# Layer 1 of a two-layer graph network: the gathered rows are added to the edge attributes by the transfer itself

## The reference, cut to what matters

```python
m = node_feat[src] + edge_feat                      # 200000 x 128
neigh = jax.ops.segment_sum(m, dst, num_segments=N)
h = 2.0 * node_feat + neigh
h = h @ W1 + b1
h = jnp.where(h > 0, h, 0.01 * h)
x = _layernorm(x + h @ W2 + b2)
```

## Time and profile before

| | us |
|---|---|
| median of 3 runs | 5750.64 (5744.35 to 5753.44) |
| span of the profiled execution, first to last instruction | 5652.3 |
| what lies around the span, if the profiled execution took the median's time | 98.3 |
| mean granted clock of PE, share of 2.4 GHz | 0.783 |

### The profile page before, as it was taken

One profiled execution on the slowest core, in us unless ns is written; L12 is line 12 of the kernel. 1 busy time (PEld: TensorE's weight loads), 2 busy tenths in 40 slices (PEclk: granted clock), 3 DMA queues, 4 the chain that ended last, 5 costly groups with the idle time before them and its releaser, 6 DMA issues. The chain is left out here.

```text
span 5652.3 us, 80469 instructions
## 1 busy us (share of the span) xinstructions
PE 3416.6 (60%) x19294; PEld 2795.9 (49%) x19295; DVE 2121.7 (38%) x8176; ACT 1585.3 (28%) x3447; POOL 2973.6 (53%) x3194
## 2 busy tenths in 40 slices
PE   5667676766666766767666455545555555555554
PEld 4455454545445544545544444445455455545454
DVE  4454554545544544545545122222222222222222
ACT  3343443334333433334333111111111111111111
POOL 2454454544554554555552656555555565555554
PEclk8787888778887878778877677777777777777777
DMA  7333333333333333333332533333333333333332
GB/s 227 81 97 89 91 94 86 93 82 92 92 88 86 94 87 86 90 85 95 91 88 59 102 91 93 92 90 93 92 92 93 92 93 92 93 91 93 92 93 70
DMA packets 459582, 525.88 MB, mean 93 GB/s; under 512 B 199115, under 2 KB 359287, under 8 KB 459551
## 3 DMA queue, kind: packets, MB, share of 16 engines
q1 hardware_dynamic: 266498, 268.35, 16.3%
q0 software_dynamic: 100352, 208.93, 15.3%
q10 hardware_dynamic: 92701, 48.23, 3.0%
HBM read 471.23 MB, written 53.95 MB: 93 GB/s over the span
## 5 line engine op out<-in xcount | busy, mean ns | idle before, releaser
L671 POOL DMA_INDIRECT rows<-xl_table,src_idx x1568 | 1482.2, 945 | 1458.0 <-DVE wmsg L1124 655.5
L1446 POOL DMA_INDIRECT rows<-x_table,src_idx x1568 | 1480.4, 944 | 1102.7 <-issue 605.8
L1491 PE MATMUL ph<-ident,relu_h 128*128 128x128 f32 x196 | 83.9, 428 | 1103.0 <-DVE relu_h L1636 726.0
L1491 PEld LDWEIGHTS ph<-ident,relu_h 128*128 128x128 f32 x196 | 33.0, 168 | 1164.0 <-DVE relu_h L1636 755.5
L703 PE MATMUL ph<-node_of,xr_win 128*128 128x512 f32 x784 | 517.8, 797 | 5.9 <-issue 5.1
L745 PE MATMUL pA<-wmsg,edge_of 128*128 128x136 f32 x3136 | 430.7, 293 | 94.9 <-issue 56.9
L911 ACT ACTIVATE relu_h<-ph 128x512 f32<-128x512 f32 x392 | 232.1, 597 | 849.3 <-PE ph L703 551.9
L1532 ACT ACTIVATE relu_h<-ph,b 128x128 f32<-128x128 f32 x196 | 72.0, 367 | 1383.6 <-PE ph L1496 1044.1
L745 PEld LDWEIGHTS pA<-wmsg,edge_of 128*128 128x128 f32 x3136 | 402.7, 199 | 104.8 <-issue 100.5
L767 PE MATMUL pA<-win,last_node 128*1 128x136 f32 x392 | 99.0, 345 | 573.7 <-ACT win L925 513.1
L729 PE MATMUL pT<-att_heads,relu_h 128*128 128x48 f32 x3136 | 383.6, 272 | 79.0 <-issue 52.5
(11 more groups left out here) (174 smaller groups left out, 6322.4 us busy)
## 6 DMA issues: line engine op xcount, KB each, us to landing
dst_row<-in_dst SPq DMA_DIRECT2D x196, 513.0 KB
dst_row<-in_edge_attr SPq DMA_DIRECT2D x195, 512.0 KB
rows<-xl_table,src_idx POOLq DMA_INDIRECT x1568
rows<-x_table,src_idx POOLq DMA_INDIRECT x1568
sums_table<-win ACTq DMA_DIRECT2D x196, 68.0 KB
xr_win<-xr_table SPq DMA_DIRECT2D x196, 64.0 KB
relu_h<-x_table SPq DMA_DIRECT2D x196, 64.0 KB
out_x<-relu_h ACTq DMA_DIRECT2D x196, 64.0 KB
```

What stands on the lines that cost most here:

```text
L671: pool.indirect_dma_start(rows[s][:, t, :], None, xl_table[:, :], bass.IndirectOffsetOnAxis(ap=src_idx[s][:, t:t + 1], axis=0))\
L1446: pool.indirect_dma_start(rows[s][:, t, 0:D], None, x1_table[:, :], bass.IndirectOffsetOnAxis(ap=src_idx[s][:, t:t + 1], axis=0))\
L1491: pe.transpose(across_bank, x1_slot[s], ident[:, :]).then_inc(S("x1_across"), 1)
```

## The change

In layer 1 the gathers write to `attr` and add to what stands there; PE multiplies only `attr`. For that POOL waits for the attributes of the group as well as for its indices. The indices are loaded one group earlier, and SP waits for the gathers that read the slot's earlier indices before it loads new ones. The indices of group 3 too are loaded at the end of layer 0.

```diff
-                for s in range(BACK):
+                for s in range(U):
                     sp.wait_ge(S(f"rows_free0{s}"), groups // U + 1)
                     sp.dma_start(src_idx[s][:, :], bass.AP(a["src"].tensor, s * G, [[T, P], [1, T]]))\
                       .then_inc(S(f"src_in1{s}"), 16)
...
+                def load_sources(g):
+                    s = g.c % U
+                    wait_alone(sp, sp_waits, S(f"gathered1{s}"), g.use(16 * T, 0))
+                    sp.dma_start(src_idx[s][:, :], bass.AP(a["src"].tensor, g.times(G), [[T, P], [1, T]]))\
+                      .then_inc(S(f"src_in1{s}"), 16)
+
                 def load(g, parts=P):
                     s = g.c % U
                     sp.wait_ge(S("neigh_summed"), g.times(1, 1))
-                    if g.at_least(BACK):
-                        sp.dma_start(src_idx[s][:, :], bass.AP(a["src"].tensor, g.times(G), [[T, P], [1, T]]))\
-                          .then_inc(S(f"src_in1{s}"), 16)
...
                 def step(g, near):
+                    if g.at_least(U - 1) and in_range(g + 1, groups):
+                        load_sources(g + 1)
...
                         wait_alone(pool, pool_waits, S(f"src_in1{s}"), j * 16 + 16)
+                        wait_alone(pool, pool_waits, S(f"attr_in{s}"), j * 16 + 16)
                         for t in range(T):
-                            pool.indirect_dma_start(rows[s][:, t, 0:D], None, x1_table[:, :],
-                                                    bass.IndirectOffsetOnAxis(ap=src_idx[s][:, t:t + 1], axis=0))\
+                            pool.indirect_dma_start(attr[s][:, t, :], None, x1_table[:, :],
+                                                    bass.IndirectOffsetOnAxis(ap=src_idx[s][:, t:t + 1], axis=0),
+                                                    compute_op=ALU.add)\
                                 .then_inc(S(f"gathered1{s}"), 16)
...
-                    for k, m in enumerate((attr[s], rows[s][:, :, 0:D])):
-                        for t in range(T):
-                            ins = pe.matmul(bank, m[:, t, :], one_hot[:, t, :], start=(k == 0 and t == 0),
-                                            stop=(k == 1 and t == T - 1))
+                    for t in range(T):
+                        ins = pe.matmul(bank, attr[s][:, t, :], one_hot[:, t, :], start=(t == 0), stop=(t == T - 1))
...
-                    wait_alone(pe, pe_waits, S(f"attr_in{s}"), g.use(16, 16))
                     wait_alone(pe, pe_waits, S(f"gathered1{s}"), g.use(16 * T, 16 * T))
```

More of the change, by code:

```diff
@@ L1378, in _ @@
                 left_over(v, "v0l", rest_steps, homes[:, spots:spots + 2], SPAN)
-        end_phase(*[f"src_in1{s}" for s in range(BACK)])
+        end_phase(*[f"src_in1{s}" for s in range(U)])
         stat = [sb(f"stat{s}", [P, 2, 12]) for s in range(R)]
```

## The result

The changed kernel took 6058.43 us (median of 4 runs, 6041.08 to 6060.18), the kernel before on the same chip 5747.5 us (5736.91 to 5753.44): ratio 1.0506, interval 1.0469 to 1.0543. It is 5% slower where 8% faster was forecast, and lies above the stated range, which ended at 5930 us. The profiled execution took 6060.18 us.

A forecast was written before the change was run, and what follows sets the result against it. It took the PE, DVE, PE chain (12.85 us a group) as bound, then POOL: start 3128 plus 196 x 10.45 = 2048, a tail to 5197, plus 98.3 around the span: 5295 us, 456 less; range 5185 to 5930.

The forecast's parts named there:

- The adding form's price on POOL: POOL's time for an adding gather in layer 1: between 0.944 and 1.42 us, the lower end taken.
- Rival 2: POOL describes three ends of each row for two: 1.42 us a gather, 13.7 us a group, 5920 us; chance 0.12.
- anything else above 5930: The bracket for all times over 5930 us, beyond the stated range; chance 0.17, shared with rival 3.
- rival 3: DMA engines don't overlap reading and adding, one round trip a gather: 16 us a group, 6370 us; chance 0.17 with its bracket.
- further issue gaps: POOL's issue idle time in layer 1 beyond 0.30 us a gather: 0.50 us a group, kept in the 10.45 us.
- Rival 1: POOL's adding instruction grows moderately, to 1.0 to 1.3 us; 157 us for each 0.1: 5340 to 5740 us; chance 0.18.
- The DMA engines' part: The gathers' queue: a second read makes 0.276 us a gather 0.41 to 0.55, hidden under POOL's 1.244.
- PE's chain: PE, DVE, PE in layer 1: 12.85 us a group falls to 7.92 or 9.86 with half the passes, under POOL's 9.95.
- Rival 4: PE stays the bound, its sum slow for a reason other than the number of passes: 5750 us, no change; chance 0.03.
- The waits: POOL's wait for attributes and SP's for `gathered1`: free with POOL as bound, except a start 19 us later.
- The 98.3 us around the span: Difference between the kernel's median time and its traced span before, added to the 5197 us span to give 5295.
- The signs named in advance: Profile after: gather ns, POOL over 70% busy, few `src_idx` waits, 16 records, PE waiting, clock under 0.76, `add` every 10.0 to 10.8 us.

The follow-up runs named there:

- add_two_sets: The kernel before with its gathers adding into their old buffer `rows`, PE still multiplying both sets: 6041.76 us, 14.84 us a group.
- forms: The changed kernel with four adding and four plain gathers a group, of 128, 64 and 32 full rows and 128 rows of 256 bytes: 5560.12 us.
- plain_one_set: The changed kernel with plain gathers to `rows`, its waits kept, PE multiplying `rows` alone: 5854.34 us, ratio 1.017 to the kernel before.
- dve_merge: The changed kernel with plain gathers to `rows`; DVE adds `rows` to `attr` before PE multiplies one set: 5782.18 us, ratio 1.0038 to the kernel before.
- narrow_rows: plain_one_set with gathered rows of 64 bytes in place of 512: 5838.07 us.
- two_sets_fill_272: The kernel before with only a POOL fill of 128 x 272 elements after each gather: 5622.17 us, ratio 0.9768.
- merge_fill_272: dve_merge with a POOL fill of 128 x 272 elements after each gather and fewer waits on fills: 5625.34 us, ratio 0.975 to the kernel before.
- merge_paced_1: dve_merge with a POOL fill of 128 x 136 elements after each gather: 5628.36 us, ratio 0.9936 to the kernel before.
- merge_paced_half: dve_merge with a POOL fill of 128 x 136 elements after every second gather: 5660.53 us.
- merge_fill_200: dve_merge with a POOL fill of 128 x 200 elements after each gather and fewer waits on fills: 5591.97 us, ratio 0.9724 to the kernel before.
- merge_sequencer: dve_merge without a fill, ten already satisfied semaphore waits before each gather on POOL: 5826.27 us.

## Why the prediction was wrong, step by step

**The adding form's price on POOL: the term that was mis-sized, and the one that decided.** The prediction bounded it by 0.944 and 1.42 us and took the lower end. It measured 1.550 us, beyond the upper end; a group of eight is 14.84 us where the forecast had 10.45, and the point of no gain, 1.31 us, was passed. Rival 2 had the place right, POOL's instruction, and the size too small: 13.7 us a group, and its 5920 us was 138 us short. The time fell into the bracket of 0.17 for "anything else above 5930", whose named cause, rival 3, didn't come. add_two_sets shows that this alone makes the time. Whether POOL's extra time is a third end to describe, as that rival said, isn't shown, and the shapes in forms speak for nothing so simple. Bytes and rows of the gather were indeed the same; that they would fix POOL's time was the error.

A second term, 0.50 us a group of further issue gaps, was kept in the forecast and left out of the rivals. With it rival 2 would have read 6018 us, and the range would have reached near what was measured. But that would have been luck: 14.84 us is 8 x (1.550 + 0.304), so the 0.50 us were nothing when POOL didn't wait. Rival 1's 5340 to 5740 us doesn't follow from its own 157 us for 0.1 either: from 5295 at 0.944 it gives 5383 to 5853.

**The DMA engines' part was right.** The adding gathers' packets are 144 each, (275968 - 1568 x 32) / 1568, where a plain one has 32 (100352 / 3136). Their time is 21.2% of 6058.3 us less 1568 x 0.276, 852 us, that is 0.543 us a gather for 0.276: twice, within the 0.41 to 0.55 of the prediction, and hidden behind POOL's 1.855. The 0.276 is the mean of both layers; the packets of 3300 to 5300 us alone give 0.249 plain and 0.547 adding, 2.2 times. The Trainium skill says of the collectives' reduce step that it reads two sources for each chunk and for that runs at about half a copy's rate (Collectives: The Full Stack, "The bandwidth ceiling"); the measured ratio is near this. The price lay on the engine that issues. Rival 3 fell.

**PE's chain: the step that failed in its reasoning.** "If the 9.86 us are in proportion to the passes" they fall to 4.93, and by the recorded 2.99 us at least to 6.87. plain_one_set and dve_merge have half the passes and groups of 13.6 and about 13.3 us. From the same rows the prediction had read that the sum comes 5.4 us after the records, and had priced this gap as PE's work. With adding gathers and all 32 passes (add_two_sets) the gap is 0.19 us in every group. So it isn't the passes; it is time in which the news of PE's end is held up while POOL issues closely spaced gathers. Rival 4 had said so (a reason other than the number of passes), got 0.03, and its reason against it, the recorded 2.99 us, wasn't one. With the price of the adding form as forecast, the change would have brought about nothing, or a loss, if these two runs stand for it: dve_merge 1.0038, plain_one_set 1.017. In the change as made this doesn't show, because its own gathers are 1.855 us apart.

**The waits were costed right, for POOL as the bound.** POOL waits for attributes once, before the first gather. The 91.9 us there are mostly the end of layer 0; the attributes' part is 17.6 us (the gather starts 17.8 us after SP's first attribute issue, 0.2 before), where the forecast had 19. That the start at 3128 was measured at 3130.6 is partly luck, since the end of layer 0 varies by more. SP's wait for `gathered1` and the earlier indices cost nothing, with the cover named. In plain_one_set, where POOL isn't the bound, POOL waits 732.8 us for attributes, mostly after a late release.

**The 98.3 us around the span don't exist.** The changed kernel's span is 1.9 us short of its execution's time, and in every profiled run of the study they are at most 2.0 us apart. So the profiled execution of before took some 5654 us, less than the median of its kernel, and the prediction's own sum should have read 5199 us, not 5295: a small error beside the others. More follows from it: the traced execution is faster than every timed one beside the changed kernel (5736.91 to 5753.44 us), so the 12.85 us a group are those of a fast execution. If all of the difference lies in layer 1, the usual pace before is some 13.3 us (an estimate: 12.85 + 94 / 196), and the loss is 1.5 us a group, not 2.0.

**The signs named in advance** came mostly true (not the 10.0 to 10.8 us from `add` to `add`): the gathers' mean ns told the rival at once, POOL was busy 84% of the stretch, no wait for `src_idx`, 16 records a group, PE waiting for the gathers, and a granted clock of 0.55 for 0.76, which is a mean just above the lower level of 1.2 GHz, after waits of some 8 us before each sum.

**What is open.** Which part of the chip POOL's gathers and PE's completion share. Shown is that the hold-up ends with POOL's run in plain_one_set and narrow_rows and doesn't depend on the bytes (narrow_rows). With one set it vanishes with distance: by the earlier of SP and DVE the release is late by 15.6 us at 90% of the groups in dve_merge (1.245 us from gather to gather), 9.8 at 1.345 and 8.8 at 1.40, and not late at all with fills of 272 columns and more. It isn't each single distance that counts, since forms has close gathers and no lag; whether it is the mean pace or what the gathers have to describe isn't separated. The kernel before has a lag too, but it doesn't always last until POOL stops: of 168 late releases 74 came while POOL was still gathering. With two sets the lag is gone at 1.855 us (add_two_sets), but 6.5 us are left at 1.45 (two_sets_fill_272). Whether the lag with two sets is the same hold-up wasn't settled. The granted clock isn't the cause: from 4000 to 4200 us it is 0.62 in plain_one_set, where PE is late, and 0.59 in merge_fill_272, where it is on time.

## What to carry to other kernels

Price an instruction on the engine that issues it before the path of the data: halving a busy engine's work by a form of transfer that costs its issuer 64% more lost 5%, because the issuer was second in line at 8 x 1.244 of 12.85 us. If the end of an engine's records and the instruction that it releases lie apart, don't divide that gap among its instructions; look at what other engines do in it, and test by making one of them slower. Here 0.34 us of idle filling after each gather made the kernel before 2.3% faster, which halving PE's sum alone did not. And look at what runs beside an instruction that is long only now and then: the merge on DVE took back 0.86 us a group from the engine that set the pace.

## What the runs showed of the hardware

- An indirect gather of 128 rows of 512 bytes took POOL 0.943 to 0.951 us plainly and 1.550 us when adding, with 32 and 144 packets and 0.276 and 0.543 us of the DMA engines' time.
- With one set of products, back-to-back gathers on POOL (one every 1.245 us) held up the release of products on PE, by 17 us in one group of ten, and in plain_one_set until 3.3 us after the last gather of the run; with a fill and 1.455 us or more between their starts no release was late (lag 0.19 us, and 3.3 to 3.8 in every fourth group from DVE's own work).
- With two sets the lag was 3.7 us in the median at 1.249 us, 6.5 at 1.455, and 0.19 with adding gathers at 1.855.
- Plain gathers of fewer rows weren't cheaper in a mixed sequence: those of 64 and 32 rows took 1.58 and 1.43 us after one of 0.95 with 128 rows.
- A plain gather that ran beside DVE's addition of two SBUF buffers (128 x 1024, 1.23 us) took 1.81 us in place of 0.951 in merge_fill_272, in all 195 cases; in dve_merge, merge_paced_1, merge_paced_half, merge_fill_200 and merge_sequencer every gather over 1.5 us overlaps such an addition too.
